# The keys' stack in 48-row loads, the deviation spread in two parts, and later waits at the history's end

## What is computed

```python
# layer 0, cross attention: features of the history, and one summary vector cc
eh = gelu(layer_norm(hist @ hist_W + hist_b, ln_g, ln_b))      # 12544 x 512
aw = softmax(gelu(eh @ ctx_W1 + ctx_b1) @ ctx_W2 + ctx_b2, over the 12544 rows)
cc = sum(eh * aw, over the rows)
kp = gelu(layer_norm(cc @ kg_W1 + kg_b1)) @ kg_W2 + kg_b2      # 16 heads x 3x3 kernels
attn = conv3x3(masked(q @ k.T), softmax(kp))                   # 128 x 128 per head
x = x + softmax(masked(attn)) @ v @ proj_W + proj_b
# then layer 0's linear attention and its mixture of experts
# layer 1, cross attention of the 128 tokens to the same history, 16 heads of 16
k = hist @ Wq.T + bq ; v = hist @ Wq.T + bq                    # 12544 x 256, once for both
x = x + concat(softmax(q_h @ k_h.T / 4) @ v_h, over heads) @ Wo.T + bo
# then layer 1's retention layer and its feed-forward
```

## Time and profile before

| | |
|---|---|
| time of three runs | 903.31, 915.29, 939.04 us (median 915.29) |
| the profiled execution | 910.28 us, its span 908.5 us |
| PE busy / weight loads busy | 849.7 us (94%) / 686.6 us (76%) |
| DVE / ACT / POOL busy | 630.8 (69%) / 549.4 (60%) / 104.1 us (11%) |
| DMA | 125.01 MB, 138 GB/s in the mean |
| mean granted clock of PE | 0.969 of full speed |
| loads of keys into the stacks | 336 of 112 KB, 5.3 us from issue to landing |
| stores of k_high and of k_low | 49 each of 256 KB, 3.4 and 3.5 us |

### The profile page before, as it was taken

One profiled execution on the slowest core, in us unless ns is written; L12 is line 12 of the kernel. 1 busy time (PEld: TensorE's weight loads), 2 busy tenths in 40 slices (PEclk: granted clock), 3 DMA queues, 4 the chain that ended last, 5 costly groups with the idle time before them and its releaser, 6 DMA issues. The chain is left out here.

```text
span 908.5 us, 21807 instructions
## 1 busy us (share of the span) xinstructions
PE 849.7 (94%) x8804; PEld 686.6 (76%) x8804; DVE 630.8 (69%) x1289; ACT 549.4 (60%) x952; POOL 104.1 (11%) x116
## 2 busy tenths in 40 slices
PE   3999999999999999968889989999999999999988
PEld 3988888888888888836777853677777777777776
DVE  3555667777767677787964459996799898992242
ACT  2776778787787786872822110665677667778421
POOL 1322222222222222200000000000000000000000
PEclk9999999999999999997989999998899999999988
DMA  3366365546545653528219287478689999925000
GB/s 128 106 171 172 106 181 154 163 123 182 154 140 141 181 133 112 140 70 276 87 21 160 39 190 178 91 144 180 140 191 198 159 214 199 157 77 205 32 1 7
DMA packets 83141, 125.01 MB, mean 138 GB/s; under 512 B 10776, under 2 KB 73498, under 8 KB 82268
## 3 DMA queue, kind: packets, MB, share of 16 engines
q1 hardware_dynamic: 83040, 123.61, 55.3%
HBM read 84.06 MB, written 39.52 MB: 136 GB/s over the span
## 5 line engine op out<-in xcount | busy, mean ns | idle before, releaser
L1413 ACT ACTIVATE prob<-bank 128x1024 f32<-128x1024 f32 (+1 forms) x200 | 190.8, 1005 | 84.3 <-PE bank L1009 83.7
L1905 DVE TENSOR_REDUCE unit_max<-bank 128x1 f32<-128x512 f32 (+1 forms) x350 | 221.2, 675 | 29.3 <-PE bank L985 28.1
L647 PE MATMUL bank<-hc_high,w_high 128*128 128x256 f32 x392 | 115.6, 295 | 8.6 <-POOL hc_low L1473 8.4
L1570 DVE SCALAR_TENSOR_TENSOR normed<-bank,b_centered,rstd_wide 128x256 f32<-128x256 f32 x196 | 85.4, 477 | 48.3 <-ACT rstd_wide L1238 48.3
L1009 PEld LDWEIGHTS bank<-q_stack,k_stack 49*128 49x128 f32 x1568 | 105.4, 192 | 11.4 <-ACT q_stack L1405 3.2
L1024 PE MATMUL bank<-prob,vals 128*32 128x128 f32 x3136 | 111.2, 281 | 2.6 <-issue 2.5
L647 PE MATMUL bank<-hc_high,w_low 128*128 128x256 f32 x392 | 111.0, 283 | 0.0
L647 PE MATMUL bank<-hc_low,w_high 128*128 128x256 f32 x392 | 110.7, 282 | 0.0
L1009 PE MATMUL bank<-q_stack,k_stack 49*128 49x128 f32 x1568 | 105.4, 272 | 2.6 <-ACT q_stack L1405 1.1
L985 PE MATMUL bank<-k_stack,q_max 49*128 49x512 f32 (+1 forms) x400 | 100.9, 498 | 3.2 <-DVE unit_max L1905 2.7
L1024 PEld LDWEIGHTS bank<-prob,vals 128*32 128x32 f32 x3136 | 82.5, 112 | 25.9 <-issue 22.0
(11 more groups left out here) (326 smaller groups left out, 1356.2 us busy)
## 6 DMA issues: line engine op xcount, KB each, us to landing
k_stack<-k_scratch SPq DMA_DIRECT2D x336, 112.0 KB, 5.3
vals<-v_scratch SPq DMA_DIRECT2D x8, 1666.0 KB, 8.9
v_scratch<-vst SPq DMA_DIRECT2D x12, 1088.0 KB, 9.3
hc_raw<-in_ctx_t SPq DMA_DIRECT2D x49, 256.0 KB, 3.1
k_scratch<-k_high SPq DMA_DIRECT2D x49, 256.0 KB, 3.4
k_scratch<-k_low SPq DMA_DIRECT2D x49, 256.0 KB, 3.5
w_ffn<-in_l SPq DMA_DIRECT2D x4, 1920.0 KB, 13.1
w_l<-in_l SPq DMA_DIRECT2D x6, 603.0 KB, 5.4
```

What stands on the lines that cost most here:

```text
L647: last = nc.tensor.matmul(out_ap, lhs, rhs, start=(n == 0), stop=(n == len(pairs) - 1))
L1413: A(prob[:, e % NPB, :, 0:width], bank[:, at:at + 2, 0:width], ACT.Exp).then_inc(c_exp, 1)
L1570: V.scalar_tensor_tensor(out=normed[:, n // 2 % 2, c, at:at + CH], in0=bank[:, 2 * b + half, (c % 2) * CH:(c % 2 + 1) * CH], scalar=b_cent ...
L1905: V.tensor_reduce(unit_max[:, s % 2, u, hh:hh + 1], bank[:, at[hh], 0:width], AX_X, ALU.max, negate=True).then_inc(c_red, 1)
```

## The change

Four things, which the diff shows in its core:

- `k_scratch` gets 768 rows instead of 2 x 256: each key row three times in a row (high, low, high), so SP stores three parts for each chunk, k_high twice. The 48 rows of a head are neighbours, in DRAM and in the stack, and one load brings them: two loads for each chunk of the stack instead of six. The ones move to rows 0 to 15 of each head's 64 (`PART_ROW` = 16 rows, filled from the one row of ones in DRAM), the row of the maximum to row 0, and the query's rows follow; the products contract 64 rows.
- The spread of the deviation: DVE splits `h_rstd` into two fp32r parts (`deviation_parts`, two steps on 128 x 2), and PE multiplies each with the identity, also cast to fp32r, four products instead of two. The steps stand ahead of the weighted sum, whose own wait for the power goes.
- The history's end: `history_done` is marked after `q_blocks` instead of ahead of it, and PE gets four `stay_awake` products ahead of xn's turn and eight ahead of its wait for `cc_wide`.
- Counts of semaphores follow (48 for 32 at the stores, 32 for 96 at a chunk of the stack).

```diff
-MAX_ROW = 32
-HEAD_ROWS = 3 * HD + 1
+MAX_ROW = 0
+PART_ROW = 16
+HEAD_ROWS = PART_ROW + 3 * HD
+KEY_STORES = 16 * 3
...
-                at = 64 * hh + d
-                high[src, q, at] = high[src, q, at + HD] = 1
-                low[src, q, at + 2 * HD + 1] = 1
+                at = 64 * hh + PART_ROW + 3 * d
+                high[src, q, at] = high[src, q, at + 1] = 1
+                low[src, q, at + 2] = 1
...
-                sp.dma_start(k_out[0, :, :, cols], k_high[:, n % 2].bitcast(F32)).then_inc(k_stored[n % 2], 16)
-                sp.dma_start(k_out[1, :, :, cols], k_low[:, n % 2].bitcast(F32)).then_inc(k_stored[n % 2], 16)
+                for part_of, src in enumerate((k_high, k_low, k_high)):
+                    sp.dma_start(k_out[part_of, :, :, cols], src[:, n % 2].bitcast(F32)).then_inc(k_stored[n % 2], 16)
...
-                for at, which in ((0, 0), (HD, 1), (2 * HD + 1, 0)):
-                    for hh in range(2):
-                        row = 2 * HD * s + HD * hh
-                        sp.dma_start(k_stack[s % 2][64 * hh + at:64 * hh + at + HD, cols].bitcast(F32),
-                                     k_scratch[which, row:row + HD, cols]).then_inc(c_stack[s % 2][c], 16)
+                for hh in range(2):
+                    row = 3 * HD * (2 * s + hh)
+                    sp.dma_start(k_stack[s % 2][64 * hh + PART_ROW:64 * hh + HEAD_ROWS, cols].bitcast(F32),
+                                 k_scratch[row:row + 3 * HD, cols]).then_inc(c_stack[s % 2][c], 16)
...
-                    row = 64 * hh + MAX_ROW
-                    sp.dma_start(k_stack[b][row:row + 1, :].bitcast(F32), ones_scratch).then_inc(c_fill[b], 16)
+                    sp.dma_start(k_stack[b][64 * hh:64 * hh + PART_ROW, :].bitcast(F32),
+                                 ones_scratch.broadcast_to([PART_ROW, S])).then_inc(c_fill[b], 16)
...
-                pe.wait_ge(h_rs, n + 1)
+                pe.wait_ge(h_rl, n + 1)
                 wait_at(pe, h_rw, n)
                 for s in range(2):
-                    last = nc.tensor.matmul(bank[:, 4, s * HB:(s + 1) * HB], h_rstd[:, s:s + 1].broadcast_to([P, P]),
-                                            ident, start=True, stop=True)
+                    for part_of in range(2):
+                        last = nc.tensor.matmul(bank[:, 4, s * HB:(s + 1) * HB],
+                                                rstd_parts[:, part_of, s:s + 1].broadcast_to([P, P]),
+                                                ident_r[:, :], start=(part_of == 0), stop=(part_of == 1))
...
             pe.wait_ge(h_nm, CT * NCH)
+            stay_awake(4, 4)
             turn("xn1", xn, "xn1_t")
...
             pe.wait_ge(ld_kg, 16)
+            stay_awake(8, 4)
             dve_s.wait(pe, "cc_wide")
...
+            def deviation_parts(n):
+                dve.wait_ge(h_rs, n + 1)
+                wait_at(dve, h_bc, n)
+                V.tensor_copy(rstd_parts[:, 0, :], h_rstd[:, :]).then_inc(h_rh, 1)
+                dve.wait_ge(h_rh, n + 1)
+                V.tensor_tensor(rstd_parts[:, 1, :], h_rstd[:, :], rstd_parts[:, 0, :].bitcast(F32),
+                                ALU.subtract).then_inc(h_rl, 1)
...
+                if 0 <= n - 1:
+                    deviation_parts(n - 1)
                 group, piece = divmod(n - 2 * GC, GC)
                 if 0 <= group:
-                    dve.wait_ge(h_rs, n)
                     weighted_sum(group, *pieces_of(group)[piece])
...
             variance(NCH - 1)
+            deviation_parts(NCH - 1)
             weighted_sum(left[0][0], *left[0][1])
...
-            for b in range(2):
-                dve.wait_ge(k_stored[b], 32 * ((NCH + 1 - b) // 2))
-                dve.wait_ge(v_stored[b], 16 * ((VG + 1 - b) // 2))
-            dve.wait_ge(pe_s.sem, 1)
-            done(V.memset(gone[:, :], 0.0), "history_done")
...
             head_blocks(q_blocks, bank[:, 1, T:2 * T], 1, "q_blocks0")
+            for b in range(2):
+                dve.wait_ge(k_stored[b], KEY_STORES * ((NCH + 1 - b) // 2))
+                dve.wait_ge(v_stored[b], 16 * ((VG + 1 - b) // 2))
+            dve.wait_ge(pe_s.sem, 1)
+            done(V.memset(gone[:, :], 0.0), "history_done")
...
-    k_scratch = nc.dram_tensor("k_scratch", (2, D, S), F32, kind="Internal").ap()
+    k_scratch = nc.dram_tensor("k_scratch", (3 * D, S), F32, kind="Internal").ap()
```

More of the change, by code:

```diff
@@ L180 @@
 DVE_STEPS = """
-hist_constants hist_weights x_parts mask var1 xn1 g_shift cc_wide history_done q_blocks0 var_kg kg_n att0_0 att0_1
+hist_constants hist_weights x_parts mask var1 xn1 g_shift cc_wide q_blocks0 history_done var_kg kg_n att0_0 att0_1
 kg_hT att0_2 att0_3 kern_shift kernels s_max0 s_max2 s_max1 probT0 s_max3 probT1
@@ L332, in build_kernel @@
         h_rstd = sb("h_rstd", [P, 2], scope=la)
+        rstd_parts = sb("rstd_parts", [P, 2, 2], F32R, scope=la)
+        ident_r = sb("ident_r", [P, P], F32R, scope=la)
         rstd_wide = sb("rstd_wide", [P, CH], scope=la)
@@ L474, in build_kernel @@
         h_bc, h_rw, h_nm, h_eh = sem("h_bc"), sem("h_rw"), sem("h_nm"), sem("h_eh")
+        h_rh, h_rl = sem("h_rh"), sem("h_rl")
         h_w1, h_hid, h_w2, h_lg = sem("h_w1"), sem("h_hid"), sem("h_w2"), sem("h_lg")
@@ L543, in load_chunk @@
                 sp.dma_start(hc_raw[:, n % 2], hist_src[:, :, n * CH:(n + 1) * CH]).then_inc(h_loaded[n % 2], 16)
-            k_out = k_scratch.rearrange("w (m p) s -> w p m s", p=P)
+            k_out = k_scratch.rearrange("(m p w) s -> w p m s", p=P, w=3)
             def store_keys(n):
@@ L982, in maximum @@
                 if u == 0 or (hi - 1) // CHUNK > (lo - 1) // CHUNK:
-                    pe.wait_ge(c_stack[s % 2][(hi - 1) // CHUNK], 96 * (s // 2 + 1))
+                    pe.wait_ge(c_stack[s % 2][(hi - 1) // CHUNK], 32 * (s // 2 + 1))
                 for hh, at in enumerate(max_banks(m)):
@@ L1525, in _ @@
             own[0] += 3
+            dve.wait_ge(ld_const, 16)
+            link(V.tensor_copy(ident_r[:, :], ident))
             done(V.memset(inv_width[:, :], 1.0 / C2), "hist_constants")
@@ L1546, in keys_parts @@
                 dve.wait_ge(c_kf, n + 1)
-                wait_at(dve, k_stored[b], 32 * (n // 2))
+                wait_at(dve, k_stored[b], KEY_STORES * (n // 2))
                 V.tensor_copy(k_high[:, b], k_full[:, b]).then_inc(c_kh, 1)
```

## The result

The changed kernel ran in 916.26 us (median of 20 runs, 912.86 to 925.46), the kernel before beside it in 915.05 us (20 runs, 897.82 to 941.4). The ratio is 1.0158, with a 95% interval of 1.0125 to 1.0191: slower by 1.6%, less than the 2% that count as a difference. The forecast was 898, with a range of 888 to 910, so it missed by 18 us and on the wrong side. The profiled execution took 913.94 us with a span of 911.8, against 910.3 and 908.5 before.

The account below looks back on a forecast made before the run. PE was taken to bound the history loop and the head attention, with a serial stretch between. From the profiled execution's 910.3 us, -7.6 (loop), -0.3 (last chunk) and -4.0 (history's end) made -11.9, so 898, range 888 to 910.

Parts of the forecast that it names:

- The spread saves 0.23 us: History loop: four fp32r products at 52.5 ns replace 0.44 us of weight loads, giving PE back 0.23 us a chunk.
- the other bound that the text named and did not take: Deviation's spread in the loop: four products at the old pace of 110 ns, nothing saved.
- The two DVE steps fit into the spare 0.52 us: History loop: two added steps take about 0.45 us from POOL's end; in 39 chunks 0.52 is free, so PE does not wait.
- DVE steps eat the gain: Rival in the loop: each step lasts 0.30 us, PE waits 0.2 us a chunk, no loop gain, 906 us; chance 0.09.
- POOL's low part follows the sum and is later by as much: History loop: POOL's low part starts after the weighted sum, which moves 0.37 us later; nobody inside the loop waits for it.
- The last chunk, -0.3 us: Loop's last chunk: weighted sum no longer runs beside POOL's power (1.60 us instead of 0.69); two steps cost 0.4; -0.3 us.
- The third key store costs nothing: History loop: 256 KB more a chunk and one more issue on SP, with DMA at half share; cost nothing.
- The history's end, -4.0 us: After the loop: dummies keep PE's clock at 1.00, moved mark delays kT; kg_h's transposes start at 422.6 instead of 426.65.
- the mark's wait is satisfied already: History's end: DVE finishes cc_wide at about 415.75 and the end mark follows at once, at 415.81.
- The key loads, 0 in the attention: Attention: two 48-row loads a chunk replace six of 16 rows, 64 rows contracted for 49; no time gained or lost.
- the rival at 920 us: Attention: loads become the bound if 48-row loads run at 161 GB/s, 3.6 us more a head, 22 us; chance 0.07.
- a stall less: Rival in the attention: shorter DMA queues avoid a 1.6 us PE halt and clock fall, 8.3 us, giving 890; chance 0.18.

Follow-up runs that it names:

- spread alone: Kernel before with only the deviation's spread in two fp32r parts; loads, stores and history's end as before: 926.01 us, ratio 1.0174.
- stack alone: Kernel before with only the keys' stack changed (third key store, 48-row loads, 16 ones rows, 64 contracted rows): 900.93 us, ratio 0.9949.
- fill alone: Kernel before with fifteen extra stack rows filled at the start but never read, products still contracting 49 rows: 907.52 us, ratio 0.9995.
- scores alone: Kernel before with 64 contracted rows in the attention's score products only, those for the maxima staying at 49: 910.03 us, ratio 1.0058.
- 64 rows alone: Kernel before with the attention's products contracting 64 rows instead of 49, loads of keys and history as before: 904.06 us, ratio 0.999.
- end alone: Kernel before with only the history's end changed (mark behind q_blocks, twelve dummy products): 911.13 us, ratio 0.9954.
- the probe: Kernel before with the attention's product mix and forced PE halts added ahead of the loop, in six sections of 49, 64 or mixed rows; whole time not compared.
- the mixed case: Added halt sections with 49 rows in the 512-column products and 64 in the 16 narrow ones: 98.4 and 97.6 us; in the kernel, 64 rows in scores only: 910.03 us.

## Why the prediction was wrong

**The spread saves 0.23 us (wrong).** The term was 39 x -0.23 = -9.0 us, from 52.5 ns a product. The step that failed is "since shape and type are the same": the shape is not the same. The products of the earlier trace rows contract 49 rows from alternating halves, the spread contracts 128 rows. At one pace the four records cost what the four before them did (0.11 us each in the earlier trace rows), the other bound that the text named and did not take. Measured: nothing instead of -9.0, and 1.5 us lost for the parts in the kernel with POOL's low part moved.

**The two DVE steps fit into the spare 0.52 us (right for 34 chunks, wrong for 15).** 0.17 and 0.16 us are the durations of the earlier trace rows, and in the later loop PE's weight loads wait 0.2 to 0.3 us in the tight chunks and not at all in the others (+0.9 us over 34 chunks). The rival "DVE steps eat the gain" asked whether each step might last 0.30 us everywhere. It asked for the wrong thing: not how long a step lasts alone, but what starts on POOL in the same moment. POOL's own next instruction after the power is the low part, 1.28 us; the step that failed is "POOL's low part follows the sum and is later by as much", which holds only from chunk 17 on. Before that the order within POOL's program puts it right at the cast. This cost 15.8 us from the first widening to the fifteenth, and 1.0 of the 1.5 us at the first (27.7 against 26.7 with the low part moved). The earlier trace rows had a possible sign of it (1.60 for 0.69), which the text used for a gain of 0.3 us in the last chunk and nowhere else.

**The last chunk, -0.3 us.** Its power took 0.69 us as forecast. The gain is too small to be told from the rest.

**The third key store costs nothing (right).** Last widening at 389.80 against 389.26 us.

**The history's end, -4.0 us (right in this pair of executions, too large as a gain).** First group 5.0 to 2.5 us, turn of kg_h at 6.9 us: step by step as written. But the 4.0 were taken against one execution. From the start of cc_wide's copy to the turn of kg_h it took 11.34 us there, while the executions of the other kernels with the old end took 8.35 to 8.5 (spread alone, stack alone, fill alone, scores alone) and 9.5 us (64 rows alone). Their clock was back at 1.00 for the scores, which took 3.84 us instead of 6.09. And "the mark's wait is satisfied already" held for that one execution only: in the other five the mark waited 1.1 to 2.75 us for a store of values, with q_blocks and so the scores behind it, longest where the 9.5 us stand. With the new end it was 7.3 us in five executions and 7.45 in a sixth. The term is worth 1 to 4 us, by where the clock happens to be and how late that store is. The moved mark without the twelve dummies took 10.0, so the dummies are worth 2.7 us beside it.

**The key loads, 0 in the attention (right on the loads, wrong on the sum).** No load became the bound, which ends the rival at 920 us; six loads or two made no difference. The wider loads were not clearly faster, though: with the DMA engines full (share 1.03) the core's loads ran at 169 GB/s (506 to 530 us) and 197 (570 to 582), where the text took 191 as a floor. What failed is the clause "the matmuls contract 64 rows for 49; the moving columns stay, so no time". It is true at full clock (median 271 ns in both), and 64 rows for 49 also change how long the clock stays low after a halt. The rival "a stall less" had the right place and price (8.3 us of the 11.7) and a wrong cause: with 64 rows halts of 1.3 to 1.6 us still came in five profiled executions of other kernels, without the fall. That the changed kernel's own profiled execution had no such halt is luck as far as the runs show, and what makes PE halt stays open. The other 3.4 us are not settled; the executions without a fall in the attention took between 306.3 and 310.4 us, and the 318.0 less 8.3 are within that.

The sum, redone with what was measured: 26.1 us too low in the loop, 11.7 too high in the attention, 0.8 in the other two pieces, together 15.2 of the 15.9 us between 898 and 913.94.

## What to carry to other kernels

Before an operation is put between two engines, look up what else starts at its moment, in every phase of the loop, on the other engines: here a cast of two numbers cost 1.1 us in the chunks where POOL began beside it and nothing elsewhere. A pace read from a row of the trace holds only for products that contract as many rows and alternate in the same way. And where a kernel's runs spread by 5%, compare the granted clock of the runs before any median: padding a contraction from 49 to 64 rows cost nothing that the ratio shows (0.999) and took away the longest runs.

## What the runs showed of the hardware

- After a halt of PE of about 1.5 us the granted clock went to 0.50 for 17, 31 and 75 us in the attention of kernels with 49 contracted rows (before, spread alone, end alone), and stayed at 1.00 through halts of 1.34, 1.09 and 1.63 us with 64; a halt of 2.05 us with 64 was followed by 10.2 us at 0.50. With the halts made by the probe: 117.0 us against 91.1 and 94.3 for the same work. Why the mixed case is nearer to 64 rows in the probe and nearer to 49 in the kernel was not tried further.
- A VectorE cast of 128x2 waits for a GpSimd subtraction that started 0.03 us earlier, 1.27 instead of 0.17 us; the VectorE subtraction right after it, 0.16 us, was never longer than 165 ns, but then POOL's subtraction had always ended, so nothing follows for it.
- A product on 128 rows is paced at 0.112 us up to 128 moving columns, in fp32r as in each pass of fp32; on halves of the rows in turn at 0.06 us.
